# A vision block on one core: first loads on two queues, the first x block in halves, idents in PE's load waits, and the projections reordered

## The chip, the cores and the metric

The kernel runs on one NeuronCore of a Trainium2 chip, with five engines that run side by side and meet at semaphores: TensorE (PE), VectorE (DVE), ScalarE (ACT), GpSimd (POOL) and SyncE (SP, which here only starts DMA transfers). The metric is device time in microseconds, the median of several executions. A profiled execution's span runs from its first to its last instruction, and its own whole time is a little longer.

## The reference, cut to what matters

```
tokens = patches(x) @ W.T + b              # 32 images, 3 channels, 36 patches of 768 values, width 256
h = concat(cls, tokens) + pos              # 37 tokens an image, 1184 in all
paths = sigmoid(h @ Wp + bp)               # 8 heads, depth 5
sim = cumprod(pq*pk + (1-pq)*(1-pk)).sum(-1) / 5      # causal mask
h = layernorm(h + softmax(sim) @ (h @ Wv) @ Wo)
n = layernorm(h) * gamma + beta
z = silu(n @ w1 + b1) @ w2 + b2            # w1, w2 = (integers - 128) * scales
out = layernorm(h + h + 0.5 * z)
```

All of it is float32; the parts that the change touches are the token projection and the order of two turned norms.

## The kernel before

Every engine has its program written out by hand; a row runs when its engine has done the rows ahead of it and its semaphores have come. Nothing is scheduled at run time.

**Start.** The weights W come in three parts `w_rows`, one for each channel of the image, and the images in six blocks `x_rows`, one for each channel c and half of the batch (blocks 0 to 2 are the first half of the images). SP starts them in the order weights 0, block 0, weights 1, block 1, weights 2, block 2, then `wvp`, the other blocks and the later weights (L242 to L255). ACT's queue takes the position rows, four small vectors, the biases (L636 to L649). For a block, DVE copies the rows into patch order, `by_patch` (L745); PE turns them with 12 transposes against an identity matrix, six for each half `ih` of the patch's rows, `turn_block` (L415); DVE copies the first six results, ACT the other six, into `xT` (`x_columns`, L751 and L658). PE also turns the weights (`turn_weight`, four transposes, L392; ACT copies them) and, in `turn_vectors` (L401 to L404), the position rows and the vectors. `project_channel(n, c)` (L430) adds channel n of a chunk of 8 images into a PSUM bank: outputs e = 0 and 1, two matmuls each. The chunks 0 and 1 of the first half are summed channel by channel, in four banks; `project(c, e)` (L439) does the two chunks of the second half later, six matmuls in one bank.

**Steps.** After that PE, ACT, DVE and POOL go through steps a = 0 to 10, one tile of three images each: `values_and_signs`, `turn_phi`, `score`, `weigh`. Into the steps are laid the token blocks b of 128 rows (the first has 32): `attention_out(b)`, DVE's `normalise(b)` and `normed(b)` with a power on POOL between, PE's `turn_normed(b)` (L520), ACT's `normed_columns(b)` (L707), and for pairs of blocks `hidden` (L540, L545) and `feed_forward_out(b, q)` with q the half of the hidden rows (L562). `TURN_AT` says at which step a norm is turned. `turn_normed(b)` waits until DVE has written the norm, and every later row of PE waits with it. The last step's norm is turned behind `weigh`, before the outputs of block `OUTS - 4` = 6.

Of the kernel before, what the change touches and what calls it, by code (L numbers as in the profile page):

```python
# [15 lines left out]
def vit_block(nc, x, tok_W, tok_b, cls_token, pos, Wp, bp, Wv, Wo, ln_gamma, ln_beta,  # L16
# [32 lines left out]

    FIRST = NTOK % 128  # L50
# [43 lines left out]
    with ExitStack() as ctx:  # L94
# [13 lines left out]
        bank_z = ps("bank_z", [128, 512])  # L108

# [71 lines left out]
        w_in = [sem(f"w_in{i}") for i in range(C)]  # L181
        x_in = [sem(f"x_in{i}") for i in range(2 * C)]
# [53 lines left out]
        def _(sp):  # L236
# [5 lines left out]
            for c in range(C):  # L242
                sp.dma_start(w_rows[:, :, c * 256:(c + 1) * 256], w_by_channel[c]).then_inc(w_in[c], 16)
                x_block(c)
# [138 lines left out]
        def _(pe):  # L383
            mm = pe.matmul

            def turn_weight(c):
                pe.wait_ge(w_in[c], 16)
                if c > 0:
                    pe.wait_ge(xT_act, c)
                for i in range(2):  # L390
                    for e in range(E2):
                        last = pe.transpose(bank_s[:, 2 + i, e * 128:(e + 1) * 128],  # L392
                                            w_rows[:, e, (2 * c + i) * 128:(2 * c + i + 1) * 128], ident[:])
                last.then_inc(wT_psum, 1)

            def turn_vectors():
                pe.wait_ge(vec_in, 16 * N_VEC_IN)
                pe.wait_ge(pos_in, 16)
                pe.wait_ge(weight_set, 5)
                for e in range(E2):  # L400
                    pe.transpose(bank_w[:, e * T:(e + 1) * T], pos_rows[:, e * 128:(e + 1) * 128], ident[0:T, 0:T])  # L401
                at = E2 * T
                pe.transpose(bank_w[:, at:at + N_VEC], vec_rows[:], ident[0:N_VEC, 0:N_VEC])
                pe.transpose(bank_w[:, at + N_VEC:at + N_VEC + 1], weight_row[:].rearrange("o i a b -> o (i a b)"),  # L404
                             ident[0:1, 0:1]).then_inc(vec_psum, 1)
# [18 lines left out]
            def project_channel(n, c):  # L424
                pe.wait_ge(wT_ready, n + 1)
                for e in range(E2):
# [8 lines left out]
            def project(c, e):  # L435
                for k in range(KT):
                    if e == 0 and c == 2 and k >= KT - 2:
# [139 lines left out]
            turn_block(2)  # L577
            project_channel(1, 1)
# [3 lines left out]
            project_channel(2, 1)  # L582
            turn_block(C + 1)
            for a in range(LAST):
                turn_phi(a)
                if there(a - 1):
# [4 lines left out]
                if a in TURN_AT:  # L591
# [9 lines left out]
                if a == 2:  # L601
                    pe.wait_ge(hT_ready, 3 * E2)
                    project(3, 0)
# [17 lines left out]
            weigh(TILES - 1)  # L621
            turn_normed(OUTS - 2)
            feed_forward_out(OUTS - 4, 0)
# [11 lines left out]
        def _(act):  # L635
            act.dma_start(pos_rows[:], pos.rearrange("o t d -> (o t) d")).then_inc(pos_in, 16)  # L636
# [101 lines left out]
        def _(dve):  # L738
# [8 lines left out]

            def x_columns(n):
# [5 lines left out]
            def position_columns():  # L754
                dve.wait_ge(vec_psum, 1)
                at = E2 * T
                dve.tensor_copy(vec_cols[:], bank_w[:, at:at + N_VEC]).then_inc(posb_step, 1)
                dve.tensor_copy(weight_col[:], bank_w[:, at + N_VEC:at + N_VEC + 1]).then_inc(vec_ready, 1)
                dve.wait_ge(posb_step, 1)
                for e in range(E2):  # L760
                    ts(posb[:, e, 1:T], bank_w[:, e * T + 1:(e + 1) * T], tokb_col[:, e:e + 1], None, ALU.add)
                    tt(posb[:, e, 0:1], bank_w[:, e * T:e * T + 1], cls_col[:, e:e + 1], ALU.add).then_inc(posb_step, 1)
# [198 lines left out]
```

## Time and profile before

| | us |
|---|---|
| median of 3 runs (172.44 to 172.88) | 172.73 |
| profiled execution, whole | 171.61 |
| its span | 169.9 |
| PE busy in the span (1141 matmul records) | 153.5 |
| DVE busy | 94.6 |
| POOL busy | 55.5 |
| ACT busy | 47.9 |
| from the last matmul's end (the residual of the last block starts at 165.27) to the end of the span | 4.6 |

PE is busy for 90% of the span, and 86% of the chain that ended last is PE. A float32 matmul is two records in these counts, a transpose one. A record's span contains the drain of the array, so records overlap: twelve of them last less than the sum of their means. The page counts a PE record as busy at whatever clock the array runs; two groups of the same shape show the clock by their lengths.

### The profile page before, as it was taken

Reading aid. Unit: us, or ns where it says so; the run is one execution under the profiler, and the core shown is the slowest. Engines: PE = TensorE matmul, PEld = TensorE weight load, DVE = VectorE, ACT = ScalarE, POOL = GpSimd, SP = SyncE. Lnnn points to the kernel's source line nnn. Section 1 sums busy time; section 2 is a strip of 40 time slices with the busy share of each in tenths; the row PEclk is TensorE's granted clock in tenths of the full one; section 3 lists DMA queues with packets and bytes.
Section 4 is the critical chain, followed back from the end, with each engine's and each line's share of the span. In section 5 each row is a group of like instructions: output and inputs, shape, how many; then the busy total and the mean of one; then the engine's idle time right before and its main releaser. Section 6 shows DMA issues by size and latency. Waiting matters only on the chain.

```text
span 169.9 us, 2988 instructions
## 1 busy us (share of the span) xinstructions
PE 153.5 (90%) x1141; PEld 121.8 (72%) x1141; DVE 94.6 (56%) x175; ACT 47.9 (28%) x105; POOL 55.5 (33%) x129
## 2 busy tenths in 40 slices
PE   0299999799989999999999999999999987999990
PEld 0177887577567798577887787887888866878870
DVE  0065146557778864857537776844767454543342
ACT  0412112524141423405135235224313311023100
POOL 5008811032062802646104434502653014440011
PEclk9999999999999999999999999999999999999999
DMA  5999999900000000000000000010000000000000
GB/s 138 237 219 232 247 317 395 372 29 4 0 2 4 4 0 4 0 4 4 4 31 0 0 31 4 0 35 0 0 31 4 33 0 0 7 28 31 0 31 31
DMA packets 5501, 10.67 MB, mean 63 GB/s; under 512 B 715, under 2 KB 4400, under 8 KB 5232
## 3 DMA queue, kind: packets, MB, share of 16 engines
q1 hardware_dynamic: 5248, 10.30, 21.1%
q10 hardware_dynamic: 240, 0.19, 0.6%
q8 instruction: 9, 0.15, 0.4%
q14 instruction: 4, 0.03, 0.1%
HBM read 9.27 MB, written 1.21 MB: 62 GB/s over the span
## 4 chain that ended last, share of the span: by engine, by line
PE 86%; DVE 4%; DMA 4%; ACT 1%; POOL 1%; issue 1%; ACTq 1%; POOLq 0%
PE bank_s L545 19%; PE bank_z L562 18%; PE bank_z L439 7%; PE bank_s L415 4%; PE bank_p L454 4%; DMA vec_rows<-in_L_ffn_ln_beta 4%; PE bank_s L482 3%; PE bank_p L455 3%; PE bank_w L496 3%; PE bank_s L540 2%; PE bank_p L430 2%; PE bank_o L511 2%; PE bank_w L562 2%; PE bank_o L512 2%; PE bank_w L500 2%; PE bank_o L520 2%
## 5 line engine op out<-in xcount | busy, mean ns | idle before, releaser
L545 PE MATMUL bank_s<-hnT,w 128*128 128x256 f32 (+1 forms) x160 | 35.2, 362 | 0.0
L562 PE MATMUL bank_z<-w,act 128*128 128x256 f32 (+1 forms) x144 | 33.3, 380 | 0.0
L545 PEld LDWEIGHTS bank_s<-hnT,w 128*128 128x128 f32 x160 | 28.9, 190 | 5.0
L562 PEld LDWEIGHTS bank_z<-w,act 128*128 128x128 f32 (+1 forms) x144 | 25.1, 181 | 4.5 <-issue 0.2
L829 DVE SCALAR_TENSOR_TENSOR act<-th,bank_s 128x512 f32<-128x512 f32 (+1 forms) x20 | 13.0, 648 | 20.2 <-ACT th L699 20.1
L340 POOL TENSOR_TENSOR rstd<-var,exponents 128x3 f32<-128x3 f32 (+1 forms) x10 | 8.9, 892 | 43.0 <-DVE var L813 43.0
L699 ACT ACTIVATE th<-bank_s 128x512 f32<-128x512 f32 (+1 forms) x20 | 11.3, 565 | 32.2 <-PE bank_s L545 32.2
L800 DVE RECIPROCAL recip<-bank_w 128x222 f32<-128x222 f32 (+1 forms) x11 | 16.5, 1496 | 1.2 <-PE bank_w L500 1.2
L439 PE MATMUL bank_z<-xT,wT 128*128 128x288 f32 x48 | 12.6, 413 | 0.0
L683 ACT ACTIVATE phi_q<-bank_p 128x222 f32<-128x222 f32 (+1 forms) x11 | 3.9, 351 | 31.1 <-PE bank_p L464 31.1
L795 DVE TENSOR_TENSOR probs<-probs,allowed 111x888 f32<-111x888 f32 (+1 forms) x11 | 11.5, 1046 | 1.9 <-ACT probs L693 1.9
L693 ACT ACTIVATE probs<-bank_s 111x888 f32<-111x888 f32 (+1 forms) x11 | 9.8, 889 | 8.9 <-PE bank_s L482 8.9
L358 POOL TENSOR_TENSOR fvar<-fmv,quarter_eps 128x1 f32<-128x1 f32 (+1 forms) x10 | 1.9, 191 | 31.2 <-DVE fmv L846 31.2
L707 ACT ACTIVATE hnT<-bank_o,vec_cols 128x128 f32<-128x128 f32 (+1 forms) x20 | 7.9, 451 | 11.1 <-PE bank_o L520 11.1
L745 DVE COPY x_pat<-x_rows 96x1536 f32<-96x1536 f32 x6 | 5.7, 951 | 9.0 <-DMA x_rows<-in_x 9.0
L822 DVE TENSOR_SCALAR n<-bank_o,mv,rstd 128x256 f32<-128x256 f32 (+1 forms) x10 | 5.4, 543 | 9.1 <-POOL rstd L340 9.1
L329 POOL TENSOR_TENSOR signs<-signs 111x8 f32<-111x8 f32 (+1 forms) x11 | 4.3, 387 | 19.1 <-ACT signs L668 19.1
L439 PEld LDWEIGHTS bank_z<-xT,wT 128*128 128x128 f32 x48 | 8.7, 190 | 2.5 <-DVE xT L751 0.3
L482 PEld LDWEIGHTS bank_s<-phi_q,phi_k 32*111 32x111 f32 (+1 forms) x176 | 5.2, 168 | 4.9 <-ACT phi_k L684 4.9
L838 DVE SCALAR_TENSOR_TENSOR res<-bank_z,carry 128x256 f32<-128x256 f32 (+1 forms) x9 | 3.8, 421 | 8.6 <-PE bank_z L562 7.2
L415 PE MATMUL bank_s<-ident,x_pat 96*128 96x96 f32 x72 | 8.2, 268 | 0.3 <-ACT wT L653 0.3
L751 DVE COPY xT<-bank_s 128x576 f32<-128x576 f32 x6 | 4.5, 755 | 6.9 <-PE bank_s L415 6.9
(110 smaller groups left out, 248.5 us busy)
## 6 DMA issues: line engine op xcount, KB each, us to landing
x_rows<-in_x SPq DMA_DIRECT2D x6, 576.0 KB, 13.4
q<-in_L_ffn_fc_q SPq DMA_DIRECT2D x2, 1024.0 KB, 20.5
s<-in_L_ffn_fc_scales SPq DMA_DIRECT2D x2, 1024.0 KB, 22.6
out<-fin SPq DMA_DIRECT2D x9, 128.0 KB, 1.7
w_rows<-in_L_tok_W SPq DMA_DIRECT2D x3, 256.0 KB, 8.1
wvp<-in_L_attn_Wv SPq DMA_DIRECT2D x1, 256.0 KB, 10.8
wo<-in_L_attn_Wo SPq DMA_DIRECT2D x1, 256.0 KB, 17.3
b<-in_L_ffn_fc_bias ACTq DMA_DIRECT2D x1, 128.0 KB, 10.3
```

Of the source, the lines that this page charges most:

```text
L340: pool.tensor_tensor(rstd3[0:w, :], var3[0:w, :], exponents[0:w, :], ALU.pow).then_inc(rstd3_ready, 1)
L415: last = pe.transpose(bank_s[:, 2 * ih + g // 3, (g % 3) * HR:(g % 3 + 1) * HR], x_pat[:, n % 2, g, ih * 128:(ih + 1) * 128], ident[0:HR, ...
L439: last = mm(bank_z[:, 0:CP], wT[:, k, e * 128:(e + 1) * 128], patches(k, c), start=(k == 0), stop=(k == KT - 1))
L482: last = mm(bank_s[0:n, i, g * R:g * R + n], phi_k[32 * i:32 * (i + 1), g, 0:n], phi_q[32 * i:32 * (i + 1), g, 0:n], start=True, stop=True)
L545: last = mm(block[:, i], w1[:, e, f * 128:(f + 1) * 128], hnT[p % 2][:, e, 0:n], start=False, stop=(i == 1 and e == E2 - 1))
L562: last = mm(z_bank(b)[0:w, 0:D], act2[:, f, in_pair(b)], w2[:, f, :], start=(f == 0), stop=(f == FB - 1))
L693: act.activation(probs[0:n, :, :, 0:n], scores[:, :, :, 0:n], ACT.Exp, scale=1.0 / DEPTH).then_inc(exp_ready, 1)
L699: act.activation(th[j % 2][:, :, 0:pair_width(p)], hidden_block(p, j), ACT.Tanh, scale=0.5).then_inc(th_ready, 1)
L707: last = act.activation(hnT[b // 2 % 2][:, e, in_pair(b)], bank_o[:, e * 128:e * 128 + w], ACT.Identity, scale=gamma_col[:, e:e + 1], bias ...
L795: tt(by_head, by_head, keep.broadcast_to([n, H, n]), ALU.mult).then_inc(probs_ready, 1)
L800: dve.reciprocal(recip[:, :, 0:n], by_group(bank_w[:, HG * R:2 * HG * R], n)).then_inc(recip_ready, 1)
L829: stt(out=act2[:, 2 * j:2 * j + 2, 0:n], in0=th[j % 2][:, :, 0:n], scalar=1.0, in1=hidden_block(p, j), op0=ALU.add, op1=ALU.mult).then_inc ...
```

## The change

On SP and ACT: weights 0 go to the head of ACT's queue. SP begins with block 0, in two transfers, rows 0 to 7 of each patch and rows 8 to 15; then weights 1, block 1, weights 2, block 2, the position rows (formerly first on ACT, now two transfers), and the rest as before. DVE copies block 0 in two halves, `by_half_patch`.

On PE: transposes of the identity matrix against itself stand before the weights (10), before the first half of block 0 (2) and before the second (3). `project_channel(0, 1)` follows (0, 0) at once; channel 1's and 2's first projection follows the transposes of its own block. `turn_vectors` moves behind `project_channel(1, 0)` and writes a spare part of a bank of `bank_s`. The last half of `project_channel(2, 1)` stands behind the first `turn_phi`. At step 2 `turn_normed(0)` stands between the fourth and fifth matmul of `project(3, 0)`; near the end `turn_normed(8)` stands behind the first half of block 6's output. DVE's order follows.

```diff
+    KEEP_BUSY = {"before the weights": 10, "before the first half": 2, "before the second half": 3}
+        vec_bank = bank_s[:, 1, 3 * HR:512]
...
 SP
-            for c in range(C):
-                sp.dma_start(w_rows[...c...], w_by_channel[c]).then_inc(w_in[c], 16)
-                x_block(c)
+            for ih in range(2):
+                sp.dma_start(x_rows[:, 0, ih * HALF_PATCH:(ih + 1) * HALF_PATCH], top[:, :, ih]).then_inc(x0_in[ih], 16)
+            weight_part(1)
+            x_block(1)
+            weight_part(2)
+            x_block(2)
+            sp.dma_start(pos_rows[0:32], pos_flat[0:32]).then_inc(pos_in, 16)
+            sp.dma_start(pos_rows[32:T], pos_flat[32:T]).then_inc(pos_in, 16)
...
 ACT
-            act.dma_start(pos_rows[:], pos.rearrange("o t d -> (o t) d")).then_inc(pos_in, 16)
+            act.dma_start(w_rows[:, :, 0:256], w_by_channel[0]).then_inc(w_in[0], 16)
...
 PE
+            def keep_busy(when):
+                for i in range(KEEP_BUSY[when]):
+                    pe.transpose(bank_z[:, (i % 4) * 128:(i % 4 + 1) * 128], ident[:], ident[:])
...
             def turn_vectors():
-                pe.wait_ge(pos_in, 16)
+                pe.wait_ge(pos_in, 2 * 16)
+                pe.wait_ge(xT_dve, 2)
...
             def turn_block(n):
-                pe.wait_ge(x_pat_ready, n + 1)
                 for ih in range(2):
+                    if n == 0:
+                        keep_busy("before the second half" if ih else "before the first half")
+                    pe.wait_ge(x_pat_ready, n + 2 if n > 0 else ih + 1)
+                    if n == 2 and ih == 0:
+                        pe.wait_ge(posb_step, 1 + E2)
...
+            keep_busy("before the weights")
             turn_weight(0)
-            turn_vectors()
             turn_block(0)
             project_channel(0, 0)
+            project_channel(0, 1)
             turn_weight(1)
             turn_block(1)
-            pe.wait_ge(posb_step, E2)
-            pe.wait_ge(vec_ready, 1)
-            project_channel(0, 1)
+            project_channel(1, 0)
+            turn_vectors()
             turn_weight(2)
-            project_channel(1, 0)
+            project_channel(1, 1)
             turn_block(2)
-            project_channel(1, 1)
             project_channel(2, 0)
             turn_block(C)
             values_and_signs(0)
-            project_channel(2, 1)
             turn_block(C + 1)
+            project_channel(2, 1, outputs=(0,))
             for a in range(LAST):
                 turn_phi(a)
+                if a == 0:
+                    project_channel(2, 1, outputs=(1,))
...
-                if a in TURN_AT:
+                if a in TURN_AT and a != 2:
                     turn_normed(TURN_AT[a])
...
-                    project(3, 0)
+                    project(3, 0, turn=TURN_AT[a])      # turns before the fifth of its six matmuls
...
             weigh(TILES - 1)
+            feed_forward_out(OUTS - 4, 0)
             turn_normed(OUTS - 2)
-            feed_forward_out(OUTS - 4, 0)
             feed_forward_out(OUTS - 4, 1)
...
 DVE
-            by_patch(0)
+            by_half_patch(0)
+            by_half_patch(1)
             x_columns(0)
-            position_columns()
             by_patch(1)
-            class_tokens()
             x_columns(1)
             by_patch(2)
+            position_columns()
             x_columns(2)
+            class_tokens()
             by_patch(C)
             tokens(0, 0)
             tokens(0, 1)
             x_columns(C)
             by_patch(C + 1)
             products(0)
+            x_columns(C + 1)
             tokens(1, 0)
+            by_patch(C + 2)
             tokens(1, 1)
-            x_columns(C + 1)
-            by_patch(C + 2)
```

PE's row from its first instruction, before (L392 turns weights, L401 to L404 the vectors, L415 a block; L430 projects into `bank_p` and `bank_o` for chunk 0, `bank_z` and `bank_w` for chunk 1):

```order
L392 MATMUL bank_s<-ident,w_rows 128x128 x4
L401 MATMUL bank_w<-ident,pos_rows 128x37 x2
L403 MATMUL bank_w<-ident,vec_rows 128x8
L404 MATMUL bank_w<-ident,weight_row 128x1
L415 MATMUL bank_s<-ident,x_pat 128x96 x12
L430 MATMUL bank_p<-xT,wT 128x288 x2
L430 MATMUL bank_o<-xT,wT 128x288 x2
L392 MATMUL bank_s<-ident,w_rows 128x128 x4
L415 MATMUL bank_s<-ident,x_pat 128x96 x12
L430 MATMUL bank_z<-xT,wT 128x288 x2
L430 MATMUL bank_w<-xT,wT 128x288 x2
```

The same place after (L403 the identity against itself, L411 weights, L439 a block, L454 projections):

```order
L403 MATMUL bank_z<-ident 128x128 x10
L411 MATMUL bank_s<-ident,w_rows 128x128 x4
L403 MATMUL bank_z<-ident 128x128 x2
L439 MATMUL bank_s<-ident,x_pat 128x96 x6
L403 MATMUL bank_z<-ident 128x128 x3
L439 MATMUL bank_s<-ident,x_pat 128x96 x6
L454 MATMUL bank_p<-xT,wT 128x288 x2
L454 MATMUL bank_o<-xT,wT 128x288 x2
L454 MATMUL bank_z<-xT,wT 128x288 x2
L454 MATMUL bank_w<-xT,wT 128x288 x2
L411 MATMUL bank_s<-ident,w_rows 128x128 x4
L439 MATMUL bank_s<-ident,x_pat 128x96 x12
```

The vectors are gone from the front, chunk 1's projection stands ahead of weights 1, and fifteen identity transposes have come in.

PE's row from the third weight part on, before:

```order
L392 MATMUL bank_s<-ident,w_rows 128x128 x4
L430 MATMUL bank_p<-xT,wT 128x288 x2
L430 MATMUL bank_o<-xT,wT 128x288 x2
L415 MATMUL bank_s<-ident,x_pat 128x96 x12
L430 MATMUL bank_z<-xT,wT 128x288 x2
L430 MATMUL bank_w<-xT,wT 128x288 x2
L430 MATMUL bank_p<-xT,wT 128x288 x2
L430 MATMUL bank_o<-xT,wT 128x288 x2
L415 MATMUL bank_s<-ident,x_pat 128x96 x12
```

After, from the projection of channel 1 on (L421 to L424 are the vectors):

```order
L454 MATMUL bank_p<-xT,wT 128x288 x2
L454 MATMUL bank_o<-xT,wT 128x288 x2
L421 MATMUL bank_s<-ident,pos_rows 128x37 x2
L423 MATMUL bank_s<-ident,vec_rows 128x8
L424 MATMUL bank_s<-ident,weight_row 128x1
L411 MATMUL bank_s<-ident,w_rows 128x128 x4
L454 MATMUL bank_z<-xT,wT 128x288 x2
L454 MATMUL bank_w<-xT,wT 128x288 x2
L439 MATMUL bank_s<-ident,x_pat 128x96 x12
L454 MATMUL bank_p<-xT,wT 128x288 x2
L454 MATMUL bank_o<-xT,wT 128x288 x2
L439 MATMUL bank_s<-ident,x_pat 128x96 x12
```

The vectors now stand between channel 1's first projection and weights 2, and chunk 0's projections follow the block they need without another projection between.

PE's row behind the last `weigh`, before (`n2_0` is the norm of block 8, L562 the feed-forward output):

```order
L500 MATMUL bank_w<-probs,ones_keys 32x2x74 x4
L520 MATMUL bank_o<-ident,n2_0 128x128 x2
L562 MATMUL bank_z<-w2,act2 128x256 x8
L511 MATMUL bank_o<-wo,ctxT 128x256
L512 MATMUL bank_o<-wo,ctxT 128x256
```

After (L526 is the end of `weigh`, L546 the turned norm, L588 the output):

```order
L526 MATMUL bank_w<-probs,ones_keys 32x2x74 x4
L588 MATMUL bank_z<-w2,act2 128x256 x4
L546 MATMUL bank_o<-ident,n2_0 128x128 x2
L588 MATMUL bank_z<-w2,act2 128x256 x4
L537 MATMUL bank_o<-wo,ctxT 128x256
L538 MATMUL bank_o<-wo,ctxT 128x256
```

The four matmuls of the first half now stand ahead of the turned norm, four behind it.

## Rows read from the trace of the kernel before

**Rows 1.** What PE waited for: engine, line and releaser, us in total, times, longest.

```profile
PE bank_s L392 <- DMA w_rows<-in_L_tok_W: 5.7, 1, 5.7
PE bank_o L520 <- DVE n L822: 2.5, 2, 1.9
PE bank_w L401 <- DMA vec_rows<-in_L_ffn_ln_beta: 2.1, 1, 2.1
PE bank_s L482 <- ACT phi_k L684: 1.1, 1, 1.1
```

**Rows 2.** Timeline of PE, first 45 us: start, us, engine, line, operation [idle before].

```profile
5.71 1.09 PE L392 MATMUL bank_s<-ident,w_rows 128*128 128x128 f32 x4 [5.71 <-DMA w_rows<-in_L_tok_W]
8.85 0.43 PE L401 MATMUL bank_w<-ident,pos_rows 37*128 37x37 f32 x2 [2.06 <-DMA vec_rows<-in_L_ffn_ln_beta]
...
9.51 2.18 PE L415 MATMUL bank_s<-ident,x_pat 96*128 96x96 f32 x12
11.67 1.89 PE L430 MATMUL bank_p<-xT,wT 128*128 128x288 f32 x4
...
15.75 0.69 PE L415 MATMUL bank_s<-ident,x_pat 96*128 96x96 f32 x6 [0.28 <-ACT wT L653]
...
18.24 0.60 PE L392 MATMUL bank_s<-ident,w_rows 128*128 128x128 f32 x4
18.68 1.14 PE L430 MATMUL bank_p<-xT,wT 128*128 128x288 f32 x4
...
20.62 1.16 PE L415 MATMUL bank_s<-ident,x_pat 96*128 96x96 f32 x12
...
30.57 0.36 PE L464 MATMUL bank_p<-ident,phi 111*128 111x111 f32 x2
32.06 0.66 PE L482 MATMUL bank_s<-phi_q,phi_k 32*111 32x111 f32 x16 [1.13 <-ACT phi_k L684]
```

**Rows 3.** Windows: stretch, us, busy of five engines, PEclk, DMA share, GB/s.

```profile
2.00:4.00 2.00, 0.00 (x0) 0.00 (x0) 0.00 (x0) 0.00 (x0) 1.15 (x15) 1.00 0.89 237
4.00:6.00 2.00, 0.29 (x2) 0.32 (x3) 0.00 (x0) 1.28 (x1) 0.00 (x0) 1.00 1.01 258
```

**Rows 4.** DMA issues: what, count, KB each, us to landing.

```profile
x_rows<-in_x SPq DMA_DIRECT2D x6, 576.0 KB, 13.4
...
w_rows<-in_L_tok_W SPq DMA_DIRECT2D x3, 256.0 KB, 8.1
```

**Rows 5.** Timeline of DVE, first 45 us.

```profile
8.46 0.96 DVE L745 COPY x_pat<-x_rows 96x1536 f32<-96x1536 f32 x1 [8.46 <-DMA x_rows<-in_x]
10.77 0.76 DVE L751 COPY xT<-bank_s 128x576 f32<-128x576 f32 x1 [1.36 <-PE bank_s L415]
...
12.38 0.95 DVE L745 COPY x_pat<-x_rows 96x1536 f32<-96x1536 f32 x1 [0.19 <-DMA x_rows<-in_x]
...
16.61 0.96 DVE L745 COPY x_pat<-x_rows 96x1536 f32<-96x1536 f32 x1 [0.34 <-DMA x_rows<-in_x]
...
22.00 0.94 DVE L745 COPY x_pat<-x_rows 96x1536 f32<-96x1536 f32 x1
```

**Rows 6.** Timeline of ACT, first 45 us.

```profile
11.73 0.65 ACT L658 ACTIVATE xT<-bank_s 128x576 f32<-128x576 f32 x1 [4.30 <-PE bank_s L415]
```

**Rows 7.** Timelines of PE and DVE around the turned norm of step 2.

```profile
48.95 0.31 PE L520 MATMUL bank_o<-ident,n 32*128 32x32 f32 x2 [0.61 <-DVE n L822]
...
44.31 2.28 DVE L858 SCALAR_TENSOR_TENSOR w<-q,s 128x2048 f32<-128x2048 int32 x1
...
55.81 0.54 DVE L822 TENSOR_SCALAR n<-bank_o,mv,rstd 128x256 f32<-128x256 f32 x1 [1.00 <-POOL rstd L340]
```

**Rows 8.** Timelines of PE and DVE near the end.

```profile
127.71 1.89 PE L562 MATMUL bank_z<-w,act 128*128 128x256 f32 x8
...
141.21 0.44 PE L520 MATMUL bank_o<-ident,n 128*128 128x128 f32 x2 [1.87 <-DVE n L822]
...
140.61 0.54 DVE L822 TENSOR_SCALAR n<-bank_o,mv,rstd 128x256 f32<-128x256 f32 x1 [0.97 <-POOL rstd L340]
```

More of the change, by code:

```diff
@@ L46, in vit_block @@
     PARTS = 3
+    HALF_PATCH = PATCH * IMG // 2
+    KEEP_BUSY = {"before the weights": 10, "before the first half": 2, "before the second half": 3}
     FIRST = NTOK % 128
@@ L181, in vit_block @@
         w_in = [sem(f"w_in{i}") for i in range(C)]
+        x0_in = [sem(f"x0_in{i}") for i in range(2)]
         x_in = [sem(f"x_in{i}") for i in range(2 * C)]
@@ L240, in x_block, with weight_part @@
                 sp.dma_start(x_rows[:, n, :], src).then_inc(x_in[n], 16)
-            for c in range(C):
+            def weight_part(c):
                 sp.dma_start(w_rows[:, :, c * 256:(c + 1) * 256], w_by_channel[c]).then_inc(w_in[c], 16)
-                x_block(c)
+            top = x[0:HALF, 0].rearrange("b (g o i) w -> b g o (i w)", o=2, i=PATCH // 2)
+            for ih in range(2):
[4 more added lines that the diff above has]
+            x_block(2)
+            pos_flat = pos.rearrange("o t d -> (o t) d")
+            sp.dma_start(pos_rows[0:32], pos_flat[0:32]).then_inc(pos_in, 16)
+            sp.dma_start(pos_rows[32:T], pos_flat[32:T]).then_inc(pos_in, 16)
             sp.dma_start(wvp[:, :, 0:D], Wv.rearrange("(e p) n -> p e n", p=128)).then_inc(wvp_in, 16)
@@ L422, in patches, with project_channel @@
                 return xT[:, k, half, :, at:at + CI * GRID]
-            def project_channel(n, c):
+            def project_channel(n, c, outputs=range(E2)):
                 pe.wait_ge(wT_ready, n + 1)
-                for e in range(E2):
+                for e in outputs:
                     for k in (2 * n, 2 * n + 1):
@@ L433, in project_channel, with project @@
                         last.then_inc(tok_psum, 1)
-            def project(c, e):
+            def project(c, e, turn=None):
                 for k in range(KT):
+                    if turn is not None and k == KT - 2:
+                        turn_normed(turn)
                     if e == 0 and c == 2 and k >= KT - 2:
@@ L746, in by_patch, with by_half_patch @@
                                 x_rows[:, n, :].rearrange("p (i g j) -> p g i j", i=PATCH, g=GRID)).then_inc(x_pat_ready, 1)
+            def by_half_patch(ih):
+                dve.wait_ge(x0_in[ih], 16)
+                dve.tensor_copy(x_pat[:, 0, :, ih * 128:(ih + 1) * 128].rearrange("p g (i j) -> p g i j", i=PATCH // 2),
+                                x_rows[:, 0, ih * HALF_PATCH:(ih + 1) * HALF_PATCH].rearrange(
+                                    "p (i g j) -> p g i j", i=PATCH // 2, g=GRID)).then_inc(x_pat_ready, 1)
             def x_columns(n):
@@ L756, in position_columns @@
                 at = E2 * T
-                dve.tensor_copy(vec_cols[:], bank_w[:, at:at + N_VEC]).then_inc(posb_step, 1)
-                dve.tensor_copy(weight_col[:], bank_w[:, at + N_VEC:at + N_VEC + 1]).then_inc(vec_ready, 1)
+                dve.tensor_copy(vec_cols[:], vec_bank[:, at:at + N_VEC]).then_inc(posb_step, 1)
+                dve.tensor_copy(weight_col[:], vec_bank[:, at + N_VEC:at + N_VEC + 1]).then_inc(vec_ready, 1)
                 dve.wait_ge(posb_step, 1)
                 for e in range(E2):
-                    ts(posb[:, e, 1:T], bank_w[:, e * T + 1:(e + 1) * T], tokb_col[:, e:e + 1], None, ALU.add)
-                    tt(posb[:, e, 0:1], bank_w[:, e * T:e * T + 1], cls_col[:, e:e + 1], ALU.add).then_inc(posb_step, 1)
+                    ts(posb[:, e, 1:T], vec_bank[:, e * T + 1:(e + 1) * T], tokb_col[:, e:e + 1], None, ALU.add)
+                    tt(posb[:, e, 0:1], vec_bank[:, e * T:e * T + 1], cls_col[:, e:e + 1], ALU.add).then_inc(posb_step, 1)
             def class_tokens():
```

6 lines of the change are left out of this document (3 added, 3 removed).

## The prediction

> **What bounds the kernel now.** I read the list of what TensorE (PE) waited for first, then PE's timeline from the start to the first score, then VectorE (DVE) and ScalarE (ACT) over the same stretch. PE is busy for 153.5 of 169.9 us, and the waits say where the rest is: nothing until the first weight block lands at 5.7 us, then 2.1 us for the vectors, 1.1 us before the first score, 2.5 us for two turned norms [rows 1]. Behind the last matmul stand 4.6 us of norm and store that no edit touches. In between PE hardly stops, so whatever shortens PE's own row shortens the kernel, and whatever is moved in front of PE lengthens it.
>
> The start is worse than its idle time. The twelve transposes of the first x block took 2.18 us, the same twelve later 1.16 us; the first projection 1.89 us, a later one 1.14 us [rows 2]. Per instruction that is 0.165 against 0.083 us, a factor of two. The page prints a full granted clock for every slice, the windows too [rows 3], but these durations say that the array ran at the lower level, 1.2 GHz, until some time in that first projection. What PE had done before the rise: four transposes at 5.7 us, 2 us of nothing, then unbroken work from 8.85 us.
>
> On the other side of the first block stands its data. Two transfers come first, the weight part of 256 KB and the x block of 576 KB [rows 4]. The weights arrive at 5.71 us [rows 2], and the x block only at 8.46 us, when DVE begins its 0.96 us copy into patch order [rows 5].
>
> **The change part by part.** I count from PE's start to its second-block transposes (A), from there to the first score (B), the norm turned at step 2 (C), and the norm turned near the end (D). The sum is made on the profiled execution: span 169.9, whole time 171.61 us, 1.1 us under the median of 172.73.
>
> A. Before, PE has turned weights 0 and 1 and blocks 0 and 1 and has projected chunks 0 and 1 of channel 0 at 18.4 us, where the third weight part begins at 18.24 [rows 2] (a record's start is a little before the end of the one ahead). After, the same work is done without the vectors in front, with x block 0 in halves.
>
> Landing of the weights: bounds 3.1 us (their 262 kB alone at 237 GB/s from 2.0 us [rows 3]) and 8.46 us (no sooner than the whole x block before). I take 5.4, next to the old 5.71. Landing of the second x half: both transfers are 852 kB, and at 237, then 258 GB/s [rows 3] they are through at 5.5 us at the earliest; 8.46 at the latest. I take 6.2, as DVE must see the last of them; half a copy is 0.48, so 6.7.
>
> The ten transposes of the identity before the weights cost 0.21 us each at the lower level (four weight transposes took 1.09) and lie inside PE's 5.7 us of waiting: nothing. The two and three around the half blocks do stand in the path, 0.11 to 0.21 us each. From 5.4: at the lower level 1.09 + 0.43 + 1.0 + 0.64 + 1.0 ends the block's transposes at 9.6; at the upper level 0.60 + 0.22 + 0.5, the wait for the copy, 0.33 and 0.5 end them at 7.55. I take the middle, 8.6, against 11.69 before. ACT's copy of the second half follows (0.1 + 0.65 [rows 6]): 9.35. The first of the four matmuls of the projection ran during that; three at 0.49 end at 10.8, the four of chunk 1 (1.94) at 12.75, weights 1 (0.45) at 13.2.
>
> What is late next is x block 1. DVE began its copy at 12.38, stopped by the transfer [rows 5]; if that stays, PE gets the block at 13.35 and ends it, with the 0.28 us wait for the weights' copy [rows 2], at 14.6. So A is 18.4 - 14.6 = 3.8 us. Bounds 1.4 (below, under the clock rival) and 4.8 (x1 a microsecond sooner).
>
> B. Before, 32.06 - 18.4 = 13.65 us to the first score, of which 1.13 is idle: PE had nothing to put beside ACT's two copies of phi [rows 2]. After, half of a projection (0.97) lies there, and 0.16 of the wait is left: a gain of 0.97. Against it: the vectors, 0.73 us in front of everybody before (8.85 to 9.58), are now in PE's row at about half of that, 0.4. And the projections of channels 1 and 2 follow their own block's transposes at once, where before another projection stood between. The first matmul then waits for DVE's 0.76 us copy [rows 5], begun when the first half (0.5 us) was turned: 0.1 + 0.76 - 0.5 = 0.36 each, 0.72 together. ACT's copy is covered by that matmul. For the position rows, whose transfer now stands behind x block 2, I add 0.1: that block landed at 16.61 [rows 5], and PE comes to the vectors at about 14.6 + 0.36 + 1.94 = 16.9. B is 0.97 - 0.4 - 0.72 - 0.1 = -0.25, say -0.3, bounds -1.5 and +0.3.
>
> C. PE's 0.61 us at 48.95 go, since four matmuls of the projection now stand ahead of the norm. But the stall came from DVE, busy without a gap from 44.31 on with the weights' 2.28 us [rows 7] and then a row of copies. PE arrives 0.6 us sooner at the next turned norm, at 55.9, where DVE's `normed(1)` still ends at 55.81 + 0.54 = 56.35. So about 0.3 of 0.61 stays; bounds 0 and 0.6.
>
> D. The stall of 1.87 us [rows 8] is filled with half of a feed-forward output, eight records that took 1.73 us net (127.71 to 129.44) [rows 8]. PE is then free at 139.34 + 1.73 = 141.07, and the norm is written at 140.61 + 0.54 = 141.15: about 0.1 is left. Behind it the output of the last attention block needs ACT's copy of the turned norm, and the other half's 1.73 us hide that. So +1.7, bounds 0.9 and 1.87.
>
> Sum: 3.8 - 0.3 + 0.3 + 1.7 = 5.5 us. Span 164.4, profiled execution 166.1, median 167.2.
>
> **The rivals.**
>
> Late weights. The weight part now travels beside the x halves instead of ahead of them. From 2 us on the DMA engines' share stands at 0.89 and above [rows 3], so nothing is free to take the second queue; weights and second half may both land at 7.3. All at the lower level that ends the block's transposes at 7.3 + 4.16 = 11.5, about as before; ACT's copy at 12.2 and 1.46 + 1.94 + 0.45 + 1.27 behind it end at 17.3. A is 1.1 and the time 169.9. For it: the full share. Against it: the block's last bytes cannot be much later than before with the same bytes ahead. The Trainium skill, "DMA: Bandwidth & Descriptors", section "Issuing engines are not separate DMA queues", says that transfers started from several engines run on the same 16 and interleave, which only saves issue time. By that rule this case comes out; the full share agrees, the landing no row shows.
>
> Cold array. The identity transposes end at about 3.8 us, PE then idles until the weights come, and the clock may stay at its lower level through the first projection, as it did before after the four transposes and the 2 us gap. Block 0 ends at 9.6, three matmuls at 0.97 end at 13.3, and A is 18.4 - 17.0 = 1.4: time 169.6. The five idents in the path then only cost 1.07. The Trainium skill, "TensorE: Matmul & The Clock Gate", Part 1, has the lower level as the default, lifted by sustained activity and lost in idleness; the durations of [rows 2] agree with the first, and whether such a gap loses it no row shows.
>
> Norms that give nothing. If DVE's chain simply moves the two stalls elsewhere, C and D are 0: 169.2. The gapless DVE speaks for it in C; in D nothing else waits on it.
>
> The slower one: PE's row now contains the wait for the position rows in its middle, with all projections, the turning of weights 2 and the rest of the kernel queued behind it. Their transfer is seventh in the first queue. The price is its landing minus 16.9; from 16.9 + 5.5 = 22.4 us on the kernel is slower than before, and a landing at 24 us gives 174.3. Against it: x block 3, further back in that queue, was in its copy at 22.00 without having been waited for [rows 5].
>
> **How the numbers follow.** Forecast 0.67, late weights 0.10, cold array 0.14, empty norms 0.05, the slower one 0.04. The forecast's own range is 165.4 (A 4.8, B 0, D 1.8) to 168.5; to keep no more than 2 in 10 out, the range goes to the late weights: 165.4 to 169.9. A measurement of this kernel tells 0.3%, 0.5 us, from no change. Every case but the last is over that: faster 0.94, same 0.02, slower 0.04.
>
> **What would show it.** PE's wait for the weights ends near 5.4, a second x copy ends near 6.7, the second six transposes take 0.5 to 1.0 us, block 1 is turned by 14.6. The first score starts near 28.6 instead of 32.06, with no wait over 0.2 in front. At step 3 PE waits some 0.3 us for `normed(1)`, and near the end 0.1 instead of 1.87. A first score before 27 or after 31, or a wait at the vectors over 1 us, would prove the sum wrong.

## The result, and the profile after

The changed kernel takes 166.29 us (median of 4 runs, 166.18 to 166.47) against 172.81 us of the kernel before beside it (172.44 to 173.25): the ratio is 0.9636, with a 95% interval of 0.9602 to 0.9671. The forecast was 167.2 us, within 165.4 to 169.9. The profiled executions stand at 166.23 (span 164.5) and 171.61 us (span 169.9), 5.4 us apart by their spans; the forecast sum was 5.5. The medians lie 6.5 us apart, since the profiled execution of before was one of its quicker ones; e1 and e4 below show where its runs differ. A single execution that takes far longer than the others is left out of the ratios and their intervals (in e6 one of 405.74 us; the other five have a median of 166.02).

First again what PE waited for (engine, line, releaser: us in all, times, longest):

```profile
PE bank_z L403 <- POOL ident L286: 1.7, 1, 1.7
PE bank_s L439 <- DVE x_pat L777: 0.7, 2, 0.4
PE bank_p L454 <- DVE xT L784: 0.4, 1, 0.4
PE bank_s L439 <- ACT wT L680: 0.3, 1, 0.3
PE bank_o L546 <- DVE n L855: 0.2, 1, 0.2
PE bank_s L439 <- DVE x_pat L772: 0.2, 1, 0.2
```

Of [rows 1] the weights, the vectors, phi and nearly all of the norms are gone. New are three small waits for DVE's copies, and 1.7 us for the identity matrix, which hold up only the idents. PE's timeline shows the new start (start us, us, engine, line, what, count, idle before and its releaser):

```profile
1.66 2.40 PE L403 MATMUL bank_z<-ident 128*128 128x128 f32 x10 [1.66 <-POOL ident L286]
3.85 1.06 PE L411 MATMUL bank_s<-ident,w_rows 128*128 128x128 f32 x4
...
5.62 0.72 PE L439 MATMUL bank_s<-ident,x_pat 96*128 96x96 f32 x6 [0.29 <-DVE x_pat L777]
...
7.04 0.71 PE L439 MATMUL bank_s<-ident,x_pat 96*128 96x96 f32 x6 [0.37 <-DVE x_pat L777]
7.80 1.45 PE L454 MATMUL bank_p<-xT,wT 128*128 128x288 f32 x4
...
13.37 0.69 PE L439 MATMUL bank_s<-ident,x_pat 96*128 96x96 f32 x6 [0.28 <-ACT wT L680]
14.03 1.52 PE L454 MATMUL bank_p<-xT,wT 128*128 128x288 f32 x4
15.39 1.13 PE L454 MATMUL bank_o<-xT,wT 128*128 128x288 f32 x4
16.45 0.31 PE L421 MATMUL bank_s<-ident,pos_rows 37*128 37x37 f32 x2
...
19.34 1.15 PE L439 MATMUL bank_s<-ident,x_pat 96*128 96x96 f32 x12
20.94 1.21 PE L454 MATMUL bank_p<-xT,wT 128*128 128x288 f32 x4 [0.45 <-DVE xT L784]
...
25.33 1.21 PE L439 MATMUL bank_s<-ident,x_pat 96*128 96x96 f32 x12 [0.18 <-DVE x_pat L772]
...
28.64 0.66 PE L508 MATMUL bank_s<-phi_q,phi_k 32*111 32x111 f32 x16
...
52.79 0.44 PE L546 MATMUL bank_o<-ident,n 128*128 128x128 f32 x2 [0.25 <-DVE n L855]
...
137.58 0.44 PE L546 MATMUL bank_o<-ident,n 128*128 128x128 f32 x2
```

Six transposes of the first half block take 0.72 us, where twelve took 2.18 [rows 2]: the array is at 2.4 GHz before the first projection, not in the middle of it. The trace also records when the granted clock changes, from its first change on (the views print 1.00 for the time before it): it rises to the upper level at 5.24 us here and at 13.06 us in before. Block 1 is turned and both chunks of channel 0 are projected by 14.03 us, a state that before reached at 18.24. The first score stands at 28.64 instead of 32.06 and waits for nothing, and the norm near the end finds its data there. On DVE the two halves and the next block come as follows (8.46 and 12.38 before [rows 5]):

```profile
5.01 0.56 DVE L777 COPY x_pat<-x_rows 96x768 f32<-96x768 f32 x1 [5.01 <-DMA x_rows<-in_x]
6.43 0.56 DVE L777 COPY x_pat<-x_rows 96x768 f32<-96x768 f32 x1 [0.86 <-DMA x_rows<-in_x]
...
10.57 0.96 DVE L772 COPY x_pat<-x_rows 96x1536 f32<-96x1536 f32 x1 [2.92 <-DMA x_rows<-in_x]
```

From 2 to 4 us the DMA engines moved more than in [rows 3], 300 against 237 GB/s (last columns: PEclk, DMA share, GB/s):

```profile
2.00:4.00 2.00, 2.00 (x11) 1.93 (x10) 0.00 (x0) 0.00 (x0) 1.14 (x15) 1.00 0.96 300
```

### The profile page after: what moved, and what is told of

Its sections match the earlier page's. It is cut to its first block, busy times and chain, and to the rows that moved or that the text cites. A ratio compares the mean times of both kernels' runs of the same rounds, so it can differ in the third digit from the quotient of the medians.

```text
span 164.5 us, 3024 instructions
## 1 busy us (share of the span) xinstructions
PE 156.2 (95%) x1156; PEld 122.8 (75%) x1156; DVE 94.7 (58%) x176; ACT 48.0 (29%) x105; POOL 54.7 (33%) x129
## 4 chain that ended last, share of the span: by engine, by line
PE 83%; DVE 6%; DMA 3%; POOL 3%; issue 2%; SPq 0%; ACT 0%; POOLq 0%
PE bank_s L571 19%; PE bank_z L588 19%; PE bank_z L465 5%; PE bank_p L480 3%; PE bank_s L508 3%; DMA x_rows<-in_x 3%; PE bank_s L439 3%; PE bank_w L522 3%; PE bank_s L566 3%; PE bank_p L454 2%; PE bank_p L481 2%; PE bank_o L537 2%; PE bank_w L588 2%; PE bank_o L538 2%; PE bank_w L526 2%; PE bank_z L454 2%
## 5 line engine op out<-in xcount | busy, mean ns | idle before, releaser
L588 PE MATMUL bank_z<-w,act 128*128 128x256 f32 (+1 forms) x144 | 33.6, 381 | 0.0
L588 PEld LDWEIGHTS bank_z<-w,act 128*128 128x128 f32 (+1 forms) x144 | 25.1, 182 | 4.7 <-issue 0.4
L439 PE MATMUL bank_s<-ident,x_pat 96*128 96x96 f32 x72 | 7.5, 250 | 1.1 <-DVE x_pat L777 0.7
L439 PEld LDWEIGHTS bank_s<-ident,x_pat 96*128 96x128 f32 x72 | 6.4, 141 | 2.6 <-DVE x_pat L777 1.3
L350 POOL TENSOR_TENSOR signs<-signs 111x16 f32<-111x16 f32 (+1 forms) x11 | 8.0, 726 | 0.9
L480 PE MATMUL bank_p<-wvp,hT 128*111 128x296 f32 (+1 forms) x22 | 8.2, 453 | 0.0
```

What stands on the lines that cost most here:

```text
L480: mm(bank_p[0:n, 0:D + HD], hT[:, 0, columns(t)], wvp[:, 0, :], start=True, stop=False)
L588: last = mm(z_bank(b)[0:w, 0:D], act2[:, f, in_pair(b)], w2[:, f, :], start=(f == 0), stop=(f == FB - 1))
```

## The experiments

Each was timed in five rounds, with the kernel before on the same chip: 172.76 us for e1 to e4, 172.88 for e5 to e8, 172.4 for e9 to e11. Where a result is set against the changed kernel, that one's 166.29 us comes from its own runs, beside a before of 172.81. Each has one profiled execution, and its rows show what happened in that one. Three dots in an edit or among rows stand for lines that are not shown.

**e1: the moved norms alone**, in the kernel before.

```
-                if a in TURN_AT:
+                if a in TURN_AT and a != 2:
...
-                    project(3, 0)
+                    project(3, 0, turn=TURN_AT[a])
...
-            turn_normed(OUTS - 2)
             feed_forward_out(OUTS - 4, 0)
+            turn_normed(OUTS - 2)
```

> The kernel before with only the two turned norms moved (C and D), its start untouched. My theory: the stall of 1.87 us near the end is filled, the one of 0.61 us mostly comes back at the next norm: 1.9 us less than before, about 170.9 us, first score unchanged at 32.1 us. Rival (both stalls only move, since VectorE sets the pace there): no change, 172.8 us. Rival (both stalls go whole): 2.4 us less, 170.4 us.

170.6 us, ratio 0.9875 (0.984 to 0.9911): 2.2 us less. Of the 2.5 us of norm waits one of 0.3 is left, the foretold one at the next norm. The rival that DVE only passes the stalls on falls; the other one (170.4 us, both stalls go whole) lies inside the interval, and only the wait that is left speaks against it. The first score was expected unchanged at 32.1 us and came at 33.58 in the profiled execution, its slowest (171.19 us). That shows why runs of before can differ. This is the same code at the start as in [rows 2], where the first group of matmuls took 1.89 and the second 1.13:

```profile
11.94 2.26 PE L430 MATMUL bank_p<-xT,wT 128*128 128x288 f32 x4
13.98 2.07 PE L430 MATMUL bank_o<-xT,wT 128*128 128x288 f32 x4
```

The clock rose here one group later, at 15.88 us instead of 13.06, which costs 1.3 us.

**e2: the changed kernel without idents.**

```
-    KEEP_BUSY = {"before the weights": 10, "before the first half": 2, "before the second half": 3}
+    KEEP_BUSY = {"before the weights": 0, "before the first half": 0, "before the second half": 0}
```

> The changed kernel without the fifteen identity transposes. [...] Rival (the idents only stand in the way): 0.5 us faster, 165.8 us.

168.04 us, ratio 0.974 (0.9712 to 0.9768), 1.75 more than with them. I had expected 1.0 to 2.5 us more, the projections at half speed for longer; that x block 1 comes late next and hides all of it was the alternative, and falls. The data land as in the changed kernel (DVE's first copy at 4.88 against 5.01), only the durations differ:

```profile
3.99 1.08 PE L411 MATMUL bank_s<-ident,w_rows 128*128 128x128 f32 x4 [3.99 <-DMA w_rows<-in_L_tok_W]
5.49 1.22 PE L439 MATMUL bank_s<-ident,x_pat 96*128 96x96 f32 x6 [0.41 <-DVE x_pat L777]
7.04 1.22 PE L439 MATMUL bank_s<-ident,x_pat 96*128 96x96 f32 x6 [0.32 <-DVE x_pat L777]
8.05 2.27 PE L454 MATMUL bank_p<-xT,wT 128*128 128x288 f32 x4
```

Everything to 10 us runs at half speed, and the clock rises at 11.45 us instead of 5.24. So the idents buy the clock's earlier rise and cost nothing: the block halves start within 0.15 us of the same times in both.

**e3: weights 0 at the head of the first queue**, in the changed kernel.

```
+            weight_part(0)
             for ih in range(2):
...
-            act.dma_start(w_rows[:, :, 0:256], w_by_channel[0]).then_inc(w_in[0], 16)
```

> The changed kernel with weights 0 at the head of the first queue again, ahead of the two halves of x block 0, instead of on ScalarE's queue. My theory: only the issue time is saved by the second queue, so the weights land no later, the halves some 0.4 us later, and the kernel loses 0 to 0.5 us: 166.3 to 166.8 us. Rival (the second queue carries the early landing): the second half lands near 7.5 instead of 6.4 us and the kernel loses 1.0 us or more, 167.3 us.

168.49 us, ratio 0.9761 (0.9726 to 0.9795), 2.2 more: my theory of 0 to 0.5 is wrong. The profiled execution is its slowest, 169.44 us. The halves land a microsecond later there (DVE at 6.12 and 7.41), which leaves a gap in PE; the other 2 us that this execution loses by block 1's projection (17.21 against 14.03) go with the clock, which rises at 13.11 us:

```profile
7.41 0.56 DVE L777 COPY x_pat<-x_rows 96x768 f32<-96x768 f32 x1 [0.73 <-DMA x_rows<-in_x]
...
6.73 1.22 PE L440 MATMUL bank_s<-ident,x_pat 96*128 96x96 f32 x6 [1.39 <-DVE x_pat L777]
...
9.35 2.27 PE L455 MATMUL bank_p<-xT,wT 128*128 128x288 f32 x4
11.41 1.98 PE L455 MATMUL bank_o<-xT,wT 128*128 128x288 f32 x4
```

After a 1.39 us gap the transposes and both groups of the first projection are at the lower level. Whether that is the gap or chance, e7 was to tell apart.

**e4: the position rows in two transfers**, in the kernel before, on the same queue and at the same place.

```
-                pe.wait_ge(pos_in, 16)
+                pe.wait_ge(pos_in, 2 * 16)
...
-            act.dma_start(pos_rows[:], pos.rearrange("o t d -> (o t) d")).then_inc(pos_in, 16)
+            act.dma_start(pos_rows[0:32], pos_flat[0:32]).then_inc(pos_in, 16)
+            act.dma_start(pos_rows[32:T], pos_flat[32:T]).then_inc(pos_in, 16)
```

> The kernel before with one edit: the position rows as two transfers (32 rows and 5) at the same place of ScalarE's queue. My theory: the single transfer of 37 rows delayed the blocks that share its way, so weights 0 come near 3.6 instead of 5.7 us, x block 0 near 7 instead of 8.5, x block 1 near 10.6 instead of 12.4 us, and the kernel gains 0.5 to 1.5 us: 171.3 to 172.3 us. Rival (the bytes set the pace, their order and splitting do not matter): the same landings, 172.8 us.

170.55 us, ratio 0.9901 (0.9862 to 0.994): 1.7 to 2.2 us less by the ratio's middle and the medians, over the 0.5 to 1.5 of my theory. The weights and the blocks on the *other* queue come sooner, with nothing changed there. PE's first row and DVE's first two copies:

```profile
4.17 1.09 PE L392 MATMUL bank_s<-ident,w_rows 128*128 128x128 f32 x4 [4.17 <-DMA w_rows<-in_L_tok_W]
...
6.83 0.96 DVE L747 COPY x_pat<-x_rows 96x1536 f32<-96x1536 f32 x1 [6.83 <-DMA x_rows<-in_x]
10.87 0.95 DVE L747 COPY x_pat<-x_rows 96x1536 f32<-96x1536 f32 x1
```

Before it was 5.71, 8.46 and 12.38. One transfer of 37 rows and 37 KB held up three large ones by 1.5 us and more (e1, with that transfer whole, has 6.22 and 8.74 for the first two). My sum had no term for that. The gain in time stands in the medians: the profiled execution, 171.38 us, is one of the slower ones, and in it the clock rose at 13.87 us, so that its first score, at 31.84, is only 0.2 sooner than in before.

**e5: the two exposed copies covered.** In the changed kernel the second halves of (0,1) and (1,1) go behind the next block's transposes.

```
-            project_channel(0, 1)
+            project_channel(0, 1, outputs=(0,))
             turn_weight(1)
             turn_block(1)
+            project_channel(0, 1, outputs=(1,))
...
-            project_channel(1, 1)
+            project_channel(1, 1, outputs=(0,))
             turn_block(2)
+            project_channel(1, 1, outputs=(1,))
```

> The changed kernel with the two projections of channels 0 and 1 for chunk 1 cut in two: one output half ahead of the next block's transposes, the other behind them, so that 0.97 us of matmuls stand between a block's transposes and the projection that reads them. My theory (TensorE waits 0.48 and 0.61 us there for the copies out of PSUM, and nothing else is late): 0.8 to 1.1 us less, 165.2 to 165.5 us, first score at 27.6 us instead of 28.6. Rival (x block 1 or the position rows are then late): under 0.4 us less, 166.0 us.

165.33 us (164.88 to 165.72), ratio 0.9575 (0.9539 to 0.9611), 0.96 less than the changed kernel, and the best of all. The wait for xT is gone, and behind block 1 a full-speed group follows at once:

```profile
12.32 0.69 PE L439 MATMUL bank_s<-ident,x_pat 96*128 96x96 f32 x6 [0.28 <-ACT wT L682]
12.84 1.16 PE L454 MATMUL bank_w<-xT,wT 128*128 128x288 f32 x4
13.84 1.13 PE L454 MATMUL bank_p<-xT,wT 128*128 128x288 f32 x4
...
27.41 0.66 PE L508 MATMUL bank_s<-phi_q,phi_k 32*111 32x111 f32 x16
```

**e6: e5, the norm of step 3 moved too, and x block 4 copied earlier.**

```
-                if a in TURN_AT and a != 2:
+                if a in TURN_AT and a not in (2, 3):
-                    project(3, 1)
+                    project(3, 1, turn=TURN_AT[a])
...
             by_patch(C)
+            by_patch(C + 1)
             tokens(0, 0)
...
-            by_patch(C + 1)
```

> As the run with the covered projections, and two more edits: the norm of block 1 is turned behind the fourth matmul of its projection too (step 3, where TensorE waits 0.25 us), and VectorE copies x block 4 before it adds the first tokens instead of after (TensorE waits 0.35 us for that block). My theory: 0.2 to 0.5 us less than that run, 164.8 to 165.2 us. Rival (VectorE's row is full, what is taken ahead makes the tokens or the next norm late): the same as that run.

166.22 us, ratio 0.962 (0.9583 to 0.9656): *more* than e5, by 0.7 us between 166.02 and 165.33. Yet from (0,1)'s second half to the first score it takes 28.70 - 14.49 = 14.21 us, e5 27.41 - 12.84 = 14.57, so the edits do gain 0.4 there. In the profiled executions (166.02 and 164.88 us) what is lost is lost earlier, where the program is the same as e5's. First e6, then e5:

```profile
5.38 1.22 PE L439 MATMUL bank_s<-ident,x_pat 96*128 96x96 f32 x6
...
8.35 2.27 PE L454 MATMUL bank_p<-xT,wT 128*128 128x288 f32 x4
10.42 1.37 PE L454 MATMUL bank_o<-xT,wT 128*128 128x288 f32 x4
```

```profile
5.68 0.97 PE L439 MATMUL bank_s<-ident,x_pat 96*128 96x96 f32 x6 [0.34 <-DVE x_pat L779]
...
7.71 1.45 PE L454 MATMUL bank_p<-xT,wT 128*128 128x288 f32 x4
```

The clock rose at 10.88 us against 6.26, in a start that differs by 0.3 to 0.4 us in when the half blocks landed (DVE's copies at 4.77 and 6.72 against 5.07 and 6.34). What decides it stays open, and so does whether the clock rose late in e6's other runs; from 165.74 to 166.48 us, their times all lie above e5's.

**e7: e3 with PE's gap filled**, nine idents instead of two before the first half.

```
-    KEEP_BUSY = {"before the weights": 10, "before the first half": 2, "before the second half": 3}
+    KEEP_BUSY = {"before the weights": 10, "before the first half": 9, "before the second half": 3}
```

> The run with weights 0 on the first queue, with nine identity transposes instead of two before the first half of x block 0, so that TensorE does not stand for the 1.4 us in which it waited for that half. My theory: half of that run's loss of 2.2 us was the clock, which rose only at the second projection after that gap; without the gap it rises before the block's transposes end, and the time is 166.9 to 167.6 us. Rival (all of the loss is the later landing, the idents only stand in the way): 168.5 us or more.

167.15 us, ratio 0.9676 (0.9639 to 0.9713): 1.3 of e3's 2.2 us come back. That is my theory's range, and the rival's 168.5 lies outside the interval. With the gap closed the same rows are at the upper level (the clock rises at 5.62 us), in a profiled execution that was its slowest (169.05 us) and shows the opposite further on:

```profile
6.55 0.56 DVE L777 COPY x_pat<-x_rows 96x768 f32<-96x768 f32 x1 [0.21 <-DMA x_rows<-in_x]
...
6.39 0.71 PE L440 MATMUL bank_s<-ident,x_pat 96*128 96x96 f32 x6
...
13.80 1.21 PE L440 MATMUL bank_s<-ident,x_pat 96*128 96x96 f32 x12 [1.03 <-DVE x_pat L772]
15.46 1.88 PE L455 MATMUL bank_p<-xT,wT 128*128 128x288 f32 x4 [0.45 <-DVE xT L784]
17.13 2.13 PE L455 MATMUL bank_o<-xT,wT 128*128 128x288 f32 x4
```

Behind a gap of 1.03 us for a late x block 1 and one of 0.45, two groups fall to half speed and take 1.7 us more than two at full speed (1.13 each). Here the granted clock shows it: 0.50 from 15.86 to 19.27 us. So a clock once up can be lost again in the load phase. The halves came at 5.78 and 6.55 us, in e3 at 6.12 and 7.41, with the same transfers in the same order: between these two executions the clock is not the only difference.

**e8: x block 0 as one transfer**, in the changed kernel.

```
-            for ih in range(2):
-                sp.dma_start(x_rows[:, 0, ih * HALF_PATCH:(ih + 1) * HALF_PATCH], top[:, :, ih]).then_inc(x0_in[ih], 16)
+            x_block(0)
...
-                dve.wait_ge(x0_in[ih], 16)
...
+            dve.wait_ge(x_in[0], 16)
             by_half_patch(0)
```

> The changed kernel with x block 0 as one transfer; VectorE still copies it in halves, one behind the other. My theory: the last byte lands as before near 6.4 us, both copies stand behind it (0.5 us later than the second alone), and TensorE has a gap of 1.5 us ahead of the block in which the clock may stay low: 0.5 to 2.0 us slower than the changed kernel, 166.8 to 168.3 us. Rival (the halves only move idle time): 166.3 us.

168.25 us, ratio 0.9771 (0.9725 to 0.9818): 2.0 more. The first half now waits for the whole block (DVE begins at 6.10 us), and again the rows behind the gap are at the lower level; the clock rises at 9.97 us:

```profile
6.71 1.22 PE L436 MATMUL bank_s<-ident,x_pat 96*128 96x96 f32 x6 [1.37 <-DVE x_pat L773]
```

x block 1 came at 8.99 us here, sooner than in any trace with the halves (9.49 and later): one trace, but a sign that the halves have a price further back in the queue. It went unused, since PE was late by then.

**e9: (2,1) whole, ahead of phi**, in the changed kernel.

```
-            project_channel(2, 1, outputs=(0,))
+            project_channel(2, 1)
...
-                if a == 0:
-                    project_channel(2, 1, outputs=(1,))
```

> The changed kernel with the last projection of chunk 1 whole ahead of the first turned phi, as in the kernel before, so that nothing stands beside ScalarE's copies of phi. My theory: the wait of 1.13 us before the first score comes back less what the two orders share, 0.8 to 1.1 us slower than the changed kernel, 167.1 to 167.4 us. Rival (the projection in front makes phi's products ready in time and the wait only moves): under 0.3 us, 166.3 to 166.6 us.

167.41 us, ratio 0.9717 (0.9675 to 0.976): 1.1 more by the medians, and by the spans 165.5 - 164.5 = 1.0. PE's wait for ACT's phi is back before the first score:

```profile
29.80 0.66 PE L508 MATMUL bank_s<-phi_q,phi_k 32*111 32x111 f32 x16 [0.78 <-ACT phi_k L709]
```

The half projection covered all of it. From block 1's projection to the first score it takes 29.80 - 14.35 = 15.45 us, the changed kernel 28.64 - 14.03 = 14.61: the cover is worth 0.84. The other 0.3 of this execution's loss came earlier, where the second half block landed 0.32 us later (6.75 against 6.43) with the same program.

**e10: the position rows whole at their new place**, in the changed kernel.

```
-            sp.dma_start(pos_rows[0:32], pos_flat[0:32]).then_inc(pos_in, 16)
-            sp.dma_start(pos_rows[32:T], pos_flat[32:T]).then_inc(pos_in, 16)
+            sp.dma_start(pos_rows[:], pos_flat).then_inc(pos_in, 16)
...
-                pe.wait_ge(pos_in, 2 * 16)
+                pe.wait_ge(pos_in, 16)
```

> The changed kernel with the position rows as one transfer of 37 rows at their new place, behind x block 2. My theory: behind the blocks that TensorE waits for, the slow single transfer can only make the vectors late, which TensorE reaches at 16.45 us; it lands near 16.5 and later blocks have slack, so 0 to 0.5 us slower, 166.3 to 166.8 us: of the kernel before's edit it was the place that counted. Rival (the split counts everywhere): 1.5 us slower or more, 167.8 us.

166.57 us, ratio 0.9665 (0.9623 to 0.9706), 0.3 more, which the interval does not tell from none. Behind the loads that matter, the 37-row transfer harms little. With e4, where the split alone helped at the old place, either edit removes most of the delay; at the new place no run shows a need for the split.

**e11: e6 with four idents before the first half.**

```
-    KEEP_BUSY = {"before the weights": 10, "before the first half": 2, "before the second half": 3}
+    KEEP_BUSY = {"before the weights": 10, "before the first half": 4, "before the second half": 3}
```

> The kernel with the covered projections, the moved norm of block 1 and the earlier copy, with four identity transposes instead of two before the first half of x block 0. In that kernel's profile the clock rose only during the second pair of the first projection, although TensorE had worked from 1.66 us on without a gap of over 0.15 us; the same row before block 1 in the kernel with the covered projections alone had the rise by the first block. My theory: the edits after the first block are worth 0.5 us and the clock's rise 1.5 us, so with an early rise the time is 164.3 to 164.8 us and with a late one 165.7 to 166.5 us; two more idents give an early rise. Rival (the edits after the first block cost time): 165.7 us or more with an early rise.

165.53 us, ratio 0.96 (0.9562 to 0.9638). The clock is up at the first half (5.79, 0.69 us for six; it rises at 5.84), so my 164.3 to 164.8 should have come. The median lies between that and the rival's 165.7 and meets neither. The profiled execution, its slowest (166.02 us), shows two losses. PE waited 0.77 us for the second half block. And from (0,1)'s second half to the first score it takes 28.70 - 13.46 = 15.24 us, 0.7 more than in e5: DVE, now committed to copy x block 4 first, waited 0.31 us for it and copied it in 1.42 us instead of 0.95, and the tokens came late:

```profile
24.29 0.75 PE L480 MATMUL bank_p<-wvp,hT 128*111 128x296 f32 x2 [0.79 <-DVE hT L810]
```

So the rival's mechanism is real: the earlier copy gains 0.4 in e6, where the block is there, and costs 0.7 here. The times of e5 and e11 are not told apart, as their intervals overlap; nothing shows a gain over e5.

## Why the prediction was right

The time came out 0.9 us under the forecast, and in the profiled sum 5.4 us stand against 5.5. The places are compared by the starts of the same records.

- **A, forecast 3.8, measured 18.24 - 14.03 = 4.2.** The second half of block 0 was sized about right: its copy begins at 6.43 (6.2 forecast) and ends at 6.99 (6.7). The weights were not, they were there by 3.99 (e2) instead of 5.4, which did not matter behind the later half block. Block 0 is turned at 7.80 against 8.6, since the clock was up for it and the five idents that I had put in the path fell into PE's waits for the copies (0.29 and 0.37 were left of these). "Stopped by the transfer; if that stays" was the part that failed: x block 1's copy began at 10.57, not 12.38. The step kept that landing as it was; e4 shows most of it was the position rows on the other queue, which the change moved out of the way. The forecast had treated that move as a risk only.
- **B, forecast -0.3, measured 3.42 - 4.21 = -0.8.** The wait of 1.13 for phi is gone whole, but the cover alone gave 0.84 of it (e9); the rest went with the order of the rows in front. The vectors cost 0.45 (16.45 to 16.90). The two exposed copies were mis-sized: 0.36 each was forecast. Against e5, where nothing waits, block 1's rows are later by 0.14 (13.37 to 14.03 against 12.32 to 12.84; this stands in A) and 0.36 (14.03 to 15.39 against 12.84 to 13.84), and block 2's by 0.61 (19.34 to 20.94 against 17.79 to 18.78). Left out was a wait of 0.3 for x block 4's copy, at 25.33: that copy is queued behind DVE's tokens. The position rows cost nothing. These terms add up to -0.6; the other 0.2 lies in differences of under 0.1 a row.
- **C, forecast 0.3, measured 0.2,** with the foretold wait at the next norm (0.25). By the forecast's own rows, PE there at 55.9 and the norm written at 56.35, 0.45 of the 0.61 comes back, and the term should have been 0.2. **D, forecast 1.7, measured 1.74**: from the record behind the norm of step 3 to the last feed-forward group it is 161.62 - 56.69 = 104.93 us before and 156.26 - 53.07 = 103.19 after. e1 has both alone. The rows, two of before and two of after:

```profile
56.69 3.08 PE L439 MATMUL bank_z<-xT,wT 128*128 128x288 f32 x12
161.62 3.62 PE L562 MATMUL bank_w<-w,act 128*128 128x256 f32 x16
...
53.07 3.08 PE L465 MATMUL bank_z<-xT,wT 128*128 128x288 f32 x12
156.26 3.62 PE L588 MATMUL bank_w<-w,act 128*128 128x256 f32 x16
```

The error of A and that of B cancel; that the sum came out within 0.1 us is luck to that extent, and the places and their order of size are what was right. The 0.9 us between forecast and median is not in the sum: the profiled execution of before was 1.1 us quicker than its median, and the forecast carried that distance over. The changed kernel has no such distance (166.23 and 166.29). In before it probably lies in the clock's rise, which cost e1 1.3 us more with the same start; the other runs of before left no rows to show it.

Of the rivals, late weights fall: they were there by 3.99 (e2), earlier than the forecast's 5.4. The Trainium skill's rule ("DMA: Bandwidth & Descriptors", section "Issuing engines are not separate DMA queues") would have let a second queue save only the time of issuing, 0.43 us for these weights in the trace. In e3 the second half, which has the same bytes ahead of it either way, came 1.0 us later on one queue (7.41 against 6.43). But e7, with the same transfers, has it at 6.55, inside the 6.34 to 6.97 of the seven traces that have the halves behind no weights (after, e2, e5, e6, e9 to e11), so for that half nothing beyond the rule is shown. x block 1 came at 11.69 and 12.25 in e3 and e7 and at 9.49 to 10.90 in those seven, while it was issued only 0.6 us later: a hint that the second queue gives more than issue time, from two traces. The cold array was a real danger: e2 has its price alone, 1.75 us where the rival had 2.4, and e3 and e8 pay 2.2 and 2.0 us for clock and late data together. It did not come, with PE's gaps filled down to 0.4 us. Empty norms fall with e1; for the position rows PE waits neither here nor in e10.

## What to carry to other kernels

Where a kernel starts with loads, look at what PE does in the gaps: filler work that ends just before the data come cost nothing here and gave 1.75 us, and where gaps of 1.4 us stood in front of the first block (e3, e8) the clock rose only at 13.11 and 9.97 us instead of 5.24. Filling a gap does not make sure of it: in e6 the clock rose at 10.88 us without such a gap. Look for small, oddly shaped transfers ahead of or beside the first large ones, on every queue, and put them behind. And when independent work is pulled together to start sooner, leave one piece between a block's transposes and the matmuls that need their copies: that was worth another 1.0 us (e5).

## What the runs showed of the hardware

- A 37 KB transfer in 37 rows delayed larger ones of another queue: in e4 splitting it into 32 and 5 brought the weights from 5.71 to 4.17 us, and the two blocks' copies from 8.46 and 12.38 to 6.83 and 10.87. The Trainium skill ("DMA: Bandwidth & Descriptors", section "Why a DMA increments its semaphore by 16 and not by 1") says that a transfer spreads over the largest number of engines up to 16 that divides the slowest dimension of both its sides. By that rule 37 rows go to one engine and 32 to sixteen; that every large transfer then waits for its share on that one engine is inferred. The landings agree; no row here shows the single engine.
- The moment of the clock's rise isn't fixed by the program: e5 and e6 issue the same rows up to there, their clocks rise at 6.26 and 10.88 us, and block 1 is turned 1.65 us apart. The changed kernel, e9 and e10, again with the same rows up to there, have 5.24, 6.31 and 4.54. The clock falls again too, in e7 behind gaps of 1.03 and 0.45 us (0.50 from 15.86 to 19.27), while e10 kept the upper level over a gap of 1.00. In all these traces the granted clock is recorded from its first change on, and the views print 1.00 before that, over rows that last twice as long as later ones of the same shape; there the durations are the witness.
